# A graph-attention layer on one core: the score product taken as two fp32r products, and the steps of all engines put in a new order

## The reference

```
q = (h @ Wq).reshape(n, H, DK)      # h = x, n = 10000, D = 512, H = 8 heads of DK = 64
k = (h @ Wk).reshape(n, H, DK)
v = (h @ Wv).reshape(n, H, DK)
e = einsum('ehd,ehd->eh', k[src], q[dst]) / sqrt(DK)      # the score: one number per edge and head
m = segment_max(e, dst);  ex = exp(e - m[dst]);  z = segment_sum(ex, dst)
a = segment_sum((ex / z[dst])[:, :, None] * v[src], dst).reshape(n, D)
x1 = layernorm(h + a @ Wo, ln1_g, ln1_b)
f = relu(x1 @ W1 + b1) @ W2 + b2
out = layernorm(h + layernorm(x1 + f, ln2_g, ln2_b))      # the last one without gain and bias
```

## Time and profile before

| | |
|---|---|
| time, median of 3 runs | 687.24 us (686.03 to 687.55) |
| the profiled execution's own time | 688.38 us |
| its span (first to last instruction) | 686.0 us |
| busy in the span: PE, PEld | 641.2 us (93%), 486.7 us (71%) |
| busy in the span: DVE, ACT, POOL | 579.7 us (85%), 527.7 us (77%), 401.5 us (59%) |
| mean granted TensorE clock | 0.983 of full speed |

### The profile page before, as it was taken

How to read it: one execution, slowest core, us unless ns; L and a number is a source line. 1 busy time by engine, 2 the same in 40 slices (tenths; PEclk the granted TensorE clock), 3 DMA queues, 4 the chain that set the end, 5 groups by cost and what they waited for, 6 DMA issues and landing times.

```text
span 686.0 us, 10819 instructions
## 1 busy us (share of the span) xinstructions
PE 641.2 (93%) x3498; PEld 486.7 (71%) x3498; DVE 579.7 (85%) x1391; ACT 527.7 (77%) x1140; POOL 401.5 (59%) x363
## 2 busy tenths in 40 slices
PE   3999999999999999999999999999999999989940
PEld 2787877777777777777777777777778778765520
DVE  7648778969998898898889889988998898899692
ACT  2435258996888988898798889888888999698881
POOL 7164363685776865766676677654548826645423
PEclk9999999999999999999999999999999999999985
DMA  7734144546625745584374458245554654554362
GB/s 231 219 95 120 46 122 91 165 111 147 181 61 166 169 134 135 158 175 91 135 178 127 106 159 202 53 156 127 124 134 151 151 92 150 123 107 123 108 117 90
DMA packets 37746, 91.42 MB, mean 133 GB/s; under 512 B 8346, under 2 KB 9642, under 8 KB 37690
## 3 DMA queue, kind: packets, MB, share of 16 engines
q0 software_dynamic: 31536, 82.74, 47.1%
q1 hardware_dynamic: 6154, 8.01, 4.0%
HBM read 71.20 MB, written 20.99 MB: 134 GB/s over the span
## 4 chain that ended last, share of the span: by engine, by line
PE 83%; ACT 6%; DVE 4%; issue 2%; DMA 1%; POOL 1%; SPq 0%; POOLq 0%; DVEq 0%
PE pP L962 63%; PE pF L1102 5%; PE pT L1022 5%; PE pF L1094 5%; PE pT L1058 4%; ACT squares L557 3%; DMA xs<-in_x_dram,src_idx 1%; PE pS L1029 1%; DVE rows L897 1%; ACT rows L617 1%; ACT nT L585 1%; DVE rows L891 1%; ACT sd L549 0%; POOL xs L411 0%; ACT rows L576 0%
## 5 line engine op out<-in xcount | busy, mean ns | idle before, releaser
L557 ACT ACTIVATE squares<-rows,nmean 125x512 bf16<-125x512 f32 x200 | 142.2, 713 | 40.8 <-DVE nmean L901 18.2
L415 POOL DMA_INDIRECT out_dram<-rows,node_idx x40 | 45.5, 1137 | 73.0 <-ACT rows L617 64.2
L411 POOL DMA_INDIRECT x_rows<-in_x_dram,node_idx x40 | 46.7, 1168 | 55.9 <-DVE rows L916 46.5
L472 POOL DMA_DIRECT2D x_rows<-in_L_gnn_ln_b_dram x40 | 53.1, 1405 | 27.1 <-DVE rows L820 21.3
L962 PE MATMUL pP<-wo_hi,aT_hi 128*125 128x512 f32 x160 | 66.4, 415 | 0.5 <-DVE aT_lo L847 0.5
L962 PE MATMUL pP<-xTd_hi,wq_hi 128*128 128x500 f32 x160 | 66.4, 415 | 0.0
L962 PE MATMUL pP<-xTs_hi,wv_hi 128*128 128x500 f32 x160 | 65.6, 410 | 0.0
L897 DVE SCALAR_TENSOR_TENSOR rows<-pF,rows 125x512 f32<-125x512 f32 x78 | 50.6, 686 | 17.2 <-PE pF L1102 16.4
L962 PE MATMUL pP<-xTs_hi,wk_hi 128*128 128x500 f32 x160 | 63.3, 396 | 0.0
L962 PE MATMUL pP<-xTd_lo,wq_hi 128*128 128x500 f32 x160 | 63.1, 394 | 0.0
L962 PE MATMUL pP<-wo_lo,aT_hi 128*125 128x512 f32 x160 | 63.0, 394 | 0.0
(11 more groups left out here) (197 smaller groups left out, 1761.7 us busy)
## 6 DMA issues: line engine op xcount, KB each, us to landing
x_rows<-in_L_gnn_ln_b_dram POOLq DMA_DIRECT2D x40, 512.0 KB, 6.8
dst_row<-in_dst_dram SPq DMA_DIRECT2D x9, 250.5 KB, 3.6
q<-in_L_gnn_Wq_dram SPq DMA_DIRECT2D x1, 1024.0 KB, 5.8
rows<-in_L_gnn_Wk_dram SPq DMA_DIRECT2D x1, 1024.0 KB, 7.9
rows<-in_L_gnn_Wv_dram SPq DMA_DIRECT2D x1, 1024.0 KB, 9.0
x_rows<-in_L_gnn_Wo_dram SPq DMA_DIRECT2D x8, 128.0 KB, 5.0
xd<-in_x_dram,dst_idx POOLq DMA_INDIRECT x40, 4.1
xs<-in_x_dram,src_idx POOLq DMA_INDIRECT x40, 3.7
```

The costliest lines, as they stand in the source:

```text
L411: pool.indirect_dma_start(rows, None, x, bass.IndirectOffsetOnAxis(ap=table[:, column:column + 1].bitcast(U32), axis=0), bounds_check=N - ...
L415: pool.indirect_dma_start(out, bass.IndirectOffsetOnAxis(ap=table[:, column:column + 1].bitcast(U32), axis=0), rows, None, bounds_check=N ...
L472: pool.dma_start(xr_wide[n], bass.AP(tensor=be2.tensor, offset=be2.offset, ap=[[0, P], [0, 2], [1, D]]), accum_op=ALU.add).then_inc(s[f"be ...
L557: ins = act.activation(squares[:, t, :], w[n][:, t, :], ACT.Square, bias=nmean[c][n][:, t:t + 1], accum_out=sq[c][n][:, t:t + 1])
```

## The change

The score product isn't one fp32 product any more. ACT rounds q[:, 0] into a new fp32r tile `score_part` (step SH); PE multiplies it with an fp32r copy of same_head (step SA, start of the accumulation); DVE replaces the content of the same tile by what the rounding left over (step SL, which therefore waits until SA has read the tile); PE multiplies that too and adds it (step S). The tiles same_head and weight lose their own memory and lie in `far`, so three waits are added: ACT's S waits for the first half of EX, POOL's mask for DVE's LN of the round before and, once, for the copy of same_head. Step HQ makes that copy once.

```
-                    on.wait_ge("head_done", 1)
-                    on.wait_ge("counts_kept", 1)
-                    on.wait_ge("qk_acc", 3 * i + 3)
-                    on.wait_ge("weight_exp", i)
-                    pe.matmul(pS[:, 0:EG], same_head[:, :], q[:, 0, 0:EG], start=True, stop=True).then_inc(s["score_done"], 1)
+                elif step == "SA":                                   # PE
+                    on.wait_ge("head_kept", 1)
+                    on.wait_ge("counts_kept", 1)
+                    on.wait_ge("part_hi", i + 1)
+                    on.wait_ge("weight_exp", i)
+                    pe.matmul(pS[:, 0:EG], same_head_r[:, :], score_part[:, :], start=True, stop=False).then_inc(s["part_done"], 1)
+                elif step == "S":                                    # PE
+                    on.wait_ge("part_lo", i + 1)
+                    pe.matmul(pS[:, 0:EG], same_head_r[:, :], score_part[:, :], start=False, stop=True).then_inc(s["score_done"], 1)
+                elif step == "SH":                                   # ACT
+                    on.wait_ge("qk_acc", 3 * i + 3)
+                    on.wait_ge("score_done", i)
+                    act.activation(score_part[:, :], q[:, 0, 0:EG], ACT.Copy).then_inc(s["part_hi"], 1)
+                elif step == "SL":                                   # DVE
+                    on.wait_ge("part_done", i + 1)
+                    dve.tensor_tensor(score_part[:, :], q[:, 0, 0:EG], score_part[:, :].bitcast(F32), ALU.subtract).then_inc(s["part_lo"], 1)
...
-        same_head = sb("same_head", [P, P])
+        same_head_r = sb("same_head_r", [P, P], F32R)
+        score_part = sb("score_part", [P, EG], F32R)
+        same_head = far[:, 0:P]
-        weight = sb("weight", [P, EG])
+        weight = far[:, 0:EG]
+                    on.wait_ge("head_done", 1)                       # ACT, HQ
+                    act.activation(same_head_r[:, :], same_head, ACT.Copy).then_inc(s["head_kept"], 1)
+                    on.wait_ge("decay_half", i + 1)                  # ACT, S
+                    on.wait_ge("log_taken", i)                       # POOL, mask
+                    on.wait_ge("head_kept", 1)                       # POOL, mask
```

More of the change, by code:

```diff
@@ L18 @@
 ROUNDS = 10
-PERIOD = 7684
-SLOT_PERIOD = {"N0": 7683, "N1": 7685}
+PERIOD = 7686
+SLOT_PERIOD = {"N0": 7686, "N1": 7685}
 PLAN = {
     "pe": """
[L26 to L34, removed]
@@ L48 @@
+>E1.F29 158468 150440 147513 235642 337928; <E1.F1 145376 147662 146636 228940 321966;
+<E1.F2 147080 148146 147184 229413 345223
 """,
     "act": """
[L50 to L64, removed]
@@ L71 @@
-E1.sd 133115 144208 144278 165298 250301; <E1.norm 142107 144622 144498 178944 229888;
-<E1.T 143387 145695 144586 192985 252860; >E1.T9 143386 145694 144585 219373 261698;
->E1.F19 144390 146099 145647 194884 280731; <E1.seed 143644 145883 145367 197785 271038;
-<E1.F1 144391 146100 145648 204799 289591; E1.sq 147047 147739 146670 211398 306877;
-E1.sq3 148290 149818 149937 231718 345686; <E1.z 148987 150493 150260 238408 286492
+!HQ -292183; !HK -100267; !HV -82724; !HO -40422; TXD0 -145960 -18966 126172 126863 126412;
@@ new lines @@
+TXS0 -99377 19626 131525 132045 132491; Q0 -91180 37583 132064 132607 131545; V0 33571 129062 138660 138527 166066;
+TXD1 -136215 -17215 126827 127266 126977; TXS1 -94313 22740 131930 132633 133019;
+Q1 -74513 58652 132822 132775 132717; V1 39241 136005 139158 139502 184226; TXD2 -109720 -1897 130085 131261 127773;
+TXS2 -87599 42890 132911 132990 133326; Q2 -63177 64336 133465 133975 134720; V2 72343 138719 141802 144374 205356;
+TXD3 -108161 10961 130101 131284 128516; TXS3 -74199 64356 133170 133048 133694; Q3 -26235 73556 133485 134288 135712;
@@ new lines @@
+<N0.z 152040 151759 151693 255725 434723; N1.sd 76642 138027 143447 142459 177953;
+N1.norm 82503 141706 143856 145432 192974; N1.T 100399 142622 144099 150623 209814;
+N1.seed 96209 141783 142852 150632 216870; N1.F1 105953 143530 144675 153852 220709;
+N1.sq 131569 145608 146496 157875 257943; N1.sq3 145899 148041 146875 172579 297278;
+N1.z 147417 149678 148879 175893 315106; E0.sd 129309 143204 144236 156525 243497;
+<E0.norm 132191 144150 144642 158241 223649; <E0.T 132412 144710 144996 164002 169865;
@@ new lines @@
+>E0.T9 144426 146565 130331 155134 259159; >E0.F19 146655 144305 140841 170288 269778;
+<E0.seed 133216 144891 145194 160571 256736; <E0.F1 141724 145573 145480 168709 231604;
+E0.sq 146534 146420 146789 175795 283513; E0.sq3 147551 148571 148627 179299 335227;
+E0.z 149206 149328 150416 187836 340847; E1.sd 132271 145157 145226 172406 267103;
+<E1.norm 143560 145508 145843 176996 186553; <E1.T 143723 146096 146284 179452 204990;
+>E1.T9 149132 151510 124149 225492 278221; >E1.F19 155391 161741 161126 197367 290911;
@@ L76 @@
+<E1.seed 145290 146214 146419 199254 292216; <E1.F1 145484 146615 146783 209346 310066;
+E1.sq 146808 148061 146953 223801 333340; E1.sq3 149734 150038 150809 228451 350279;
+<E1.z 149892 151446 151661 230065 331683
 """,
     "dve": """
-!CAST -289173; !FLAG -268264; !TABS -230654; !FILLI -220985; !FW -80259; !B1 -61049; !LQ -126374; !LK -80572;
-!LV -53431; !LO 76149; !CNT0 -196850; !CNT1 -177901; !CNT2 -159471; !CNT3 -151097; !CNT4 -133524; !RANK -96206;
-!DIG -200821; !LIST -85406; TXD0 -124119 -44386 125840 126473 124728; TXS0 -82312 50705 130890 131449 131257;
@@ L121 @@
[L121 to L126 removed]
+!SAVE -5873; !BIAS -53695; GXD -203893 -41468 122421 123747 124695; GXS -79275 31504 129569 129533 129903;
```

139 lines of the change are left out of this document (75 added, 64 removed).

## The result

The kernel after the change takes 691.06 us (median of 4 runs, 690.29 to 691.5); before took 686.72 us beside it. The ratio is 1.0054, 95% interval 1.0037 to 1.0072: 3.7 us slower (the two medians lie 4.3 us apart), where 685.6 us (1.6 us faster) was predicted and the range ended at 688.6. The profiled execution took 691.5 us, with a span of 689.8 us against 686.0.

The account below looks back on a forecast made before the run. The prediction took PE alone to bound the kernel from about 27 to 582 us. Its terms, -1.9 - 0.9 + 1.6 - 0.4 = -1.6 us, gave 685.6 us against the median of 687.24; range 682.9 to 688.6.

Parts of the forecast that it names:

- What bounds the kernel: From about 27 to 582 us PE alone sets the time; work added to DVE or ACT is free unless PE waits.
- SA and S, -1.9: Score product on PE: 0.22 us saved in each of rounds 1 and 3 to 8, 0.4 in round 2.
- K3's stall, -0.9: K3 on PE waits for DVE's late K0 multiplication; new order removes 0.31 us in each of three middle rounds.
- The start, +1.6: Round 0: longer score chain delays V0 by 0.9 us; E1.F2 directly behind E1.F1 loses 0.7 us.
- Rounds 8 and 9: No separate term; S's saving of 0.22 us a round was to hold in rounds 3 to 8.
- The end, -0.4: From 585 us: S's later scan is covered and ACT gains 0.4 us; bounds -1.3 to +1.3.
- The sum: -1.9 (SA and S) - 0.9 (K3) + 1.6 (start) - 0.4 (end) = -1.6 us.
- The rivals: Three other outcomes: waits hidden as well, 683.6 us (0.20); gain given back, about 686.9 (0.22); VectorE late, 689.2 (0.16).
- VectorE late at O0: Rival, chance 0.16: DVE finishes L3 late, PE waits 0.6 us at O0 in six rounds; 689.2 us.
- Given back: Rival, chance 0.22: SA waits for SH or DVE reaches SL late, and the end takes time; about 686.9 us.

## Why the prediction was wrong, point by point

**What bounds the kernel: right for the middle.** PE stands alone in the chain there. The Trainium skill (Perfetto Trace Analysis, "Identifying the Most-Contended Engine") judges TensorE by two things, the arithmetic it does as a share of its peak (MFU) and its weight loads' share of the time; by the latter VectorE is the contended engine here (71% against 85%). That more work for it would cost time was the prediction's inference from this, and no sentence of the skill says so. The trace doesn't bear it out: the stretch from K3, round 2 to V0, round 7 got 2.48 us shorter.

**SA and S, -1.9: right.** By the distances of the kernel after less those of the new order with the fp32 product, the product gives 0.23 us in round 1, 0.38 in round 2 (0.4 predicted), less than 0.1 in round 3 and 0.18 to 0.21 in each of rounds 4 to 8 (0.22 predicted): 1.6 us in all, where 1.9 was predicted. It costs 0.40 us in round 0.

**K3's stall, -0.9: right.** The new order with the fp32 product gains 1.3 us between K3, round 2 and V0, round 7: three rounds (V0 of 3 to V0 of 6) are 0.35, 0.34 and 0.33 us shorter than before, the others 0.3 together. The two terms came to 1.5 + 0.9 = 2.4 us up to V0, round 7; measured 2.48. That the sum fits so closely is luck in part: the product gave 1.2 there and the order 1.3, and the order gained elsewhere in rounds 2 and 3 and lost 0.4 us from V0, round 6 to V0, round 7, none of which was worked out.

**The start, +1.6: right for its two terms, but one was missed.** K3 to V0 of round 0: +0.89 (0.9 predicted). The product alone in the old order costs the same 0.89 there; the new order alone costs 0.48, and the product on top of it 0.40. E1.F2 behind E1.F1: +0.67 (0.7 predicted), PE idle for 1.25 us there. Together +1.35 up to K3, round 2, with what the product gives back in round 1. Missed: ROFF, which now stands between TXS0 and TXS1. It adds 1.16 us from TXS0 to Q0 (2.75 against 1.59), and K0 came 1.12 later. The working doesn't have it at all.

**Rounds 8 and 9: missed, +0.7 instead of -0.2 for S.** The new order without the product has +1.04 there, so it is the order's. For the copies of TXS in round 9 the weight loads wait 0.56 us for DVE, for K3's multiplication 0.62 us.

**The end, -0.4: the step that failed.** The working looked at H0, S's scan and ACT's table load from 585 to 598. Up to there the later scan was covered, as it said: S started 4.18 us later and V0, round 9 only 0.67 later. The 0.4 us for ACT didn't come: its table load ended at 598.67, 0.92 us later than before, when K3 of round 9 had begun 0.95 later. But the working stopped at 598. From V0, round 9 to the end of the span before took 88.4 us and after 91.5, so +3.1 instead of -0.4. It also is the prediction's own last sign of being wrong: that the stretch behind 585 us has another length by more than 1.5 us. Two things make the difference:

1. The idle matmuls in front of N0.F2: 2.05 us at E1.F2 (28.46 against 26.41 with them behind N0.F2), and 3.6 us of the time in all. In the kernel before, the same misplacement costs 4.3 us.
2. The clock, which fell where PE idled: 1.58 us in the profiled execution behind E1.F2 (63.09 against 61.51). The profile of the new order alone has the idle matmuls in the same place and the clock at 1.00 there up to 660 us, so this part comes in some executions only.

With the one edit that puts the idle matmuls behind N0.F2 this stretch takes 87.9 us, 0.5 less than before. That this is near the -0.4 is luck: it is 0.8 us lost up to E1.F2 and 1.3 us gained behind it, and the working had neither.

L3 on DVE and O0 on PE, both put later, are no part of the loss against before: behind E1.F2 the kernel before took 62.8 us, the new order with O0 late 61.5. Putting them forward takes this stretch to 59.9; O0's move alone did nothing. That is a gain which the new order had left lying.

**The sum.** Forecast and measured span differ by 5.4 us (-1.6 against +3.8). Of this 3.5 us lie in the end, 1.1 in ROFF and the start up to K0, 0.9 in rounds 8 and 9; the rest fits within 0.1. The bounds of the end term, -1.3 to +1.3, were those of two rows in the stretch I had read, and not of the stretch. PE's new queue was known to its last step, and the steps behind O3 were not followed; the range lacked that stretch.

**The rivals.** None was it. VectorE late at O0 in the middle didn't occur. "Given back" named the wrong place. Each had its mechanism in the middle rounds, where the forecast was surest, or in the end as far as it had been read; none named the idle matmuls.

**What stays open.** Whether the product is worth anything by the end. On PE's way it gains 1.2 us net by the traces of the faster chips. But on the slower ones the kernel with the fp32 product came out ahead each time: 0.9971 against 0.9992 and 0.9953 against 0.9997 beside a kernel that differs in the product alone, the intervals overlapping in the first pair and touching in the second; and 0.9975 against 0.9994 beside one in which O0 stands elsewhere too. The waits and the clock in the middle rounds, read above, fit this: in the second pair the runs with the fp32 product also show the higher mean granted clock (mostly 0.985 to 0.986 against 0.975 to 0.983). The pair was never run on a faster chip with the idle matmuls in the right place, where those waits don't occur.

## What to carry to other kernels

When a whole order is new, follow every engine's queue to its last step. The steady rounds are easy to get right and here were worth 2.5 us; the last 90 us, where PE has slack, lost 3.1. Anything tied to a step by name (here idle work, elsewhere a prefetch or a table load) moves with it: for each ask what now stands behind it. A change that adds a link between engines has to be judged together with the queue positions that it needs: the same product lost 7.9 us in the old order, and the stretch from K3, round 2 to V0, round 7 got 2.5 us back when one ACT step was moved.

## What the runs showed of the hardware that was not expected

Between 40 and 660 us the granted clock fell to half only where PE had idled shortly before, for 1.8 to 5.8 us in these profiles, but not behind every such pause: the kernel with the idle matmuls moved kept 1.00 from 630 to 637 us behind a pause of 3.18 us, and the same wait of 2.2 us in front of N0.F1 was followed by the lower level in one of two kernels with the product in the old order. At the start the spacing of the matmuls (0.42 us against 0.23) shows the lower level where the profile's clock column still says 1.00. The chip itself was worth more than the change: the kernel before took 686.7 to 688.0 us on some and 695.8 to 697.9 us on others.
